# A post-norm decoder layer on one core: the keys of the second attention spread over steps, the projection's bias moved to TensorE, and first waits moved

## What is computed

```python
x = layernorm(x + self_attention(x))            # out @ proj_w.T + proj_b
x = layernorm(x + cross_attention(x, ctx, mask)) # q = x @ Wq.T + bq; k, v from 4 x 77 context rows
x = layernorm(x + moe(x))                       # router, 8 experts, top 2, capacity 1024

# cross attention
qh, kh, vh = heads(q @ Wq.T + bq), heads(k @ Wk.T + bk), heads(v @ Wv.T + bv)
scores = qh @ kh.T / sqrt(16) + mask * NEG
out = softmax(scores) @ vh
return merge(out) @ Wo.T + bo
```

## Time and profile before

| | |
|---|---|
| runs | 1827.96, 1835.07 (median), 1846.97 us |
| profiled execution | 1830.21 us, of which its span is 1828.4 us |
| busy | PE 89%, DVE 70%, PEld 58%, ACT 55%, POOL 21% of the span |
| TensorE clock granted, mean | 0.93 of full |
| DMA | 184 MB, 101 GB/s on the mean |

### The profile page before, as it was taken

How to read it: one execution, slowest core, us unless ns; L and a number is a source line. 1 busy time by engine, 2 the same in 40 slices (tenths; PEclk the granted TensorE clock), 3 DMA queues, 4 the chain that set the end, 5 groups by cost and what they waited for, 6 DMA issues and landing times. The chain is left out here.

```text
span 1828.4 us, 36172 instructions
## 1 busy us (share of the span) xinstructions
PE 1623.4 (89%) x14816; PEld 1061.1 (58%) x14816; DVE 1278.5 (70%) x2240; ACT 1006.9 (55%) x1727; POOL 387.6 (21%) x265
## 2 busy tenths in 40 slices
PE   7869999999999999999777599869984999999990
PEld 6734444444444444444366455547763888888890
DVE  6978888888888888888177446752333677777744
ACT  5326777777777777777635267844532233333313
POOL 6550000000000000000014001101452355555521
PEclk9968999999999999999889578978996999999995
DMA  7955444443433343420238866223213244434226
GB/s 240 259 168 95 93 93 91 91 90 90 98 84 65 63 69 69 69 39 9 78 125 239 191 96 122 68 86 110 84 39 114 70 96 96 96 96 96 39 24 195
DMA packets 130388, 184.36 MB, mean 101 GB/s; under 512 B 29466, under 2 KB 93736, under 8 KB 129132
## 3 DMA queue, kind: packets, MB, share of 16 engines
q1 hardware_dynamic: 113456, 153.70, 34.0%
q0 software_dynamic: 13440, 22.07, 5.8%
q10 hardware_dynamic: 3328, 6.29, 2.1%
HBM read 115.32 MB, written 70.06 MB: 101 GB/s over the span
## 5 line engine op out<-in xcount | busy, mean ns | idle before, releaser
L734 DVE TENSOR_REDUCE att_row_max<-att_ring 128x2 f32<-128x1024 f32 x512 | 601.7, 1220 | 108.4 <-PE att_ring L799 76.4
L718 ACT ACTIVATE att_w_exp<-att_s_ps 128x512 f32<-128x512 f32 x1008 | 539.2, 598 | 210.1 <-PE att_s_ps L846 140.3
L873 PE MATMUL att_a_ps<-att_w_exp,att_v_group 128*32 128x512 f32 x2048 | 273.6, 606 | 0.8 <-ACT att_acc_sb L707 0.6
L832 PE MATMUL att_s_ps<-att_q_stack,att_k_stack 62*128 62x512 f32 x640 | 183.8, 478 | 0.0
L832 PEld LDWEIGHTS att_s_ps<-att_q_stack,att_k_stack 62*128 62x128 f32 x640 | 86.2, 184 | 122.2 <-ACT att_w_exp L718 111.9
L2357 ACT ACTIVATE ex_hid<-ex_h_ps,ex_b 128x512 f32<-128x512 f32 x128 | 87.4, 686 | 116.7 <-DVE ex_h_lo L2412 66.5
L2412 DVE TENSOR_TENSOR ex_h_lo<-ex_hid,ex_h_hi 128x512 fp32r<-128x512 f32 x128 | 138.6, 1083 | 4.4
L648 POOL COPY att_eyes<-keep_slope_eye 128x384 bf16<-128x384 bf16 x16 | 8.1, 507 | 622.6 <-PE att_s_ps L846 613.7
L2307 POOL DMA_INDIRECT x_scr<-ex_y,ex_home x60 | 100.6, 1677 | 176.0 <-DVE ex_y L2402 162.3
L846 PE MATMUL att_s_ps<-att_eyes,keep_past_bf 64*128 64x64 bf16 x3786 | 131.8, 193 | 0.0
L799 PE MATMUL att_ring<-att_k_stack,att_q_stack 60*128 60x512 f32 x640 | 125.6, 439 | 5.0 <-DVE att_row_max L734 4.1
(11 more groups left out here) (314 smaller groups left out, 3552.6 us busy)
## 6 DMA issues: line engine op xcount, KB each, us to landing
first_w_raw<-ew SPq DMA_DIRECT2D x16, 1024.0 KB
att_k_stack<-qk_scr SPq DMA_DIRECT2D x40, 256.0 KB
rows_scr<-att_zeros POOLq DMA_DIRECT2D x8, 1040.0 KB, 9.3
first_rows<-rows_scr SPq DMA_DIRECT2D x16, 520.0 KB
qk_scr<-qkv_t_lo SPq DMA_DIRECT2D x14, 512.0 KB, 4.7
qk_scr<-qkv_t_hi SPq DMA_DIRECT2D x14, 512.0 KB, 4.4
keep_k_stack<-qk_scr SPq DMA_DIRECT2D x24, 256.0 KB
att_q_stack<-qk_scr SPq DMA_DIRECT2D x20, 256.0 KB
```

Of the source, the lines that this page charges most:

```text
L718: nc.scalar.activation(w_exp[(STEPS * g.n + st) % SETS][h][:, :], score_bank(v), ACT.Exp).then_inc(exp_done, 1)
L734: nc.vector.tensor_reduce(out, ring[place.slot][:, :, :], AX.X, ALU.max).then_inc(ring_free, 1)
L832: ins = nc.tensor.matmul(score_bank(v), ks[g.buf][rows, c, j, kt * P:(kt + 1) * P], qs[g.buf][rows, j, c * CH:(c + 1) * CH], start=True, s ...
L873: ins = nc.tensor.matmul(a_ps[32 * h:32 * h + 32, :], vg[g.buf][:, kt, h * VW:h * VW + 32], w_exp[(STEPS * g.n + st) % SETS][h][:, :], sta ...
```

## The change

Five edits:

1. The projection's bias is no longer added by POOL. `proj_b` is loaded as rows 0 and 64 of a tile of 128 rows that is otherwise zero, split in hi and lo on DVE in step 0, and added by a 25th matmul per 128 tokens, ones (128 rows) times the parts. `bias_x` goes, in the attention stage too (with ACT's wait for the load of `x`).
2. Keys: two per step at the end of PE's steps 3 to 6, in the two banks of `t1_ps`; PE first waits for `x1_lo_done` of the same step. The values are made in step 8 in `r_ps`, taken in step 9; `wv` is split in step 7, the keys are shifted in steps 7 and 8. DVE does `split_keys` ahead of `residual(0)` in step 1, and the mask parts (`make_masks`) at the end of step 2. The context and its weights are loaded ahead of `x` of chunk 1.
3. The mask's tiles have 128 rows, not 64.
4. `q_out` lives on into `stage_cross`: the wait for the last query stores goes from the end of `stage_self_out` to DVE behind its 14 maxima, and to each later `load_stack`. `move_top(0)` is issued ahead of the second `load_ones`, of `load_x(0)` and of `bo`.
5. In the experts' stage the waits for `const_in` go from the head of PE's and ACT's streams to ACT behind the first `split_x` and to DVE's first `shares`.

```diff
@@ stage_attention
-            pool.tensor_tensor(lent["x"], lent["x"], lent["proj_b"].unsqueeze(1).to_broadcast([P, TPC, C]), ALU.add)
...
-            act.wait_ge(io["chunk_in"][0], 16)
@@
-KEY_BANKS = 4
-MASK_ROWS = 64
+KEY_BANKS = 2
+KEY_STEPS = range(3, 7)
+MASK_ROWS = 128
@@ load_projection
-    sp.dma_start(lent["proj_b"], io["proj_b"].partition_broadcast(P)).then_inc(lent["weights_in"], 16)
+    sp.dma_start(lent["proj_b"], io["proj_b"]).then_inc(lent["weights_in"], 16)
@@ stage_self_out, sync
-            for n in range(1, LOADED):
-                load(n)
-                if n == 1:
-                    load_keys()
...
+            sp.dma_start(att[1][:, :, :], chunk_rows(io["att_scr"], 1)).then_inc(in_done[1], 16)
+            load_keys()
+            sp.dma_start(x[1], chunk_rows(io["x"], 1)).then_inc(in_done[1], 16)
+            load(2)
+            load_masks()
+            load(3)
...
-                if n == 0:
+                if n == 3:
                     load_ones(sp, io, stacks[0], ones_in)
-                if n == 2:
+                if n == 6:
                     sp.wait_ge(k_done, PAIRS)
                     load_ones(sp, io, stacks[1], ones_in)
-                if n in (5, 7):
+                if n in (4, 6):
                     first_side(sp, n // 2 - 2, 0)
             sp.wait_ge(ones_in, 64)
             for c in range(2):
                 sp.wait_ge(x1_out[c], 16 * CHUNKS // 2)
-                sp.wait_ge(q_out[c], Q_STORES * CHUNKS // 2)
@@ gpsimd
-            def bias_x(n):
...
+            pool.memset(all_ones[:, :].bitcast(F32), 1.0).then_inc(pool_step, 1)
@@ scalar
+                if step in KEY_STEPS:
+                    for j in range(2):
+                        take_keys(2 * (step - KEY_STEPS[0]) + j)
+                if step == 7:
+                    act.wait_ge(weights_in, 112)
+                    nc.scalar.activation(wv_hi[:, :, :], wv_raw[:, :, :], ACT.Copy).then_inc(key_hi, 1)
+                if step in (7, 8):
+                    for j in range((step - 7) * PAIRS // 2, (step - 6) * PAIRS // 2):
                         shifted_keys(j)
@@ vector
+                if step == 0:
+                    dve.wait_ge(weights_in, 80)
+                    nc.vector.tensor_copy(proj_parts[:, :], proj_b).then_inc(prep, 1)
+                    dve.wait_ge(prep, 3)
+                    nc.vector.tensor_tensor(proj_parts[64:128, :], proj_b[64:128, :], proj_parts[64:128, :].bitcast(F32), ALU.subtract).then_inc(prep, 1)
+                if step == 1:
+                    split_keys()
                 if mid is not None:
                     residual(mid)
                     moments(mid)
-                if step == 1:
-                    split_keys()
...
+                if step == 2:
+                    make_masks()
+                if step in KEY_STEPS:
+                    for j in range(2):
+                        key_parts(2 * (step - KEY_STEPS[0]) + j)
@@ tensor
                              for a, b in parts3(a_hi[n % 2], a_lo[n % 2], w_hi, w_lo)]
+                    prods.append((all_ones[:, :], proj_parts[:, :]))
...
-                if step in (1, 2):
-                    for j in range((step - 1) * KEY_BANKS, step * KEY_BANKS):
-                        keys(j)
                 if old is not None:
-                    if old == 0:
-                        pe.wait_ge(k_taken, KEY_BANKS + 2)
                     transpose_x1(old)
-                if step == 2:
+                if last is not None:
+                    queries(last)
+                if step in KEY_STEPS:
+                    pe.wait_ge(x1_lo_done, old + 1)
+                    for j in range(2):
+                        keys(2 * (step - KEY_STEPS[0]) + j)
+                if step == 8:
                     for i in range(2):
                         make_values(i)
@@ stage_cross, sync
+            load_ones(sp, io, qst[2], ones_in)
             load_stack(2)
-            for i in (2, 3):
-                load_ones(sp, io, qst[i], ones_in)
+            move_top(0)
+            sp.wait_ge(ones_in, 96)
+            load_ones(sp, io, qst[3], ones_in)
             load_x(0)
-            move_top(0)
@@ vector, behind the 14 maxima
+            for c in range(2):
+                dve.wait_ge(q_out[c], Q_STORES * CHUNKS // 2)
@@ stage_experts
-            act.wait_ge(const_in, 32)
...
             split_x(0, 0)
+            act.wait_ge(const_in, 32)
...
+                if h == 0:
+                    dve.wait_ge(const_in, 32)
...
-            pe.wait_ge(const_in, 32)
```

More of the change, by code:

```diff
@@ L1040, in cross_tiles @@
             "v_all": s.sb("v_all", [L, B, H, VP], F32), "key_bias": s.sb("key_bias", [L, B], F32),
-            "stacks": [s.sb(f"q_stack{i}", [P, PAIRS, CH], F32R) for i in range(2)]}
+            "stacks": [s.sb(f"q_stack{i}", [P, PAIRS, CH], F32R) for i in range(2)],
+            "q_out": [s.sem(f"q_out{i}") for i in range(2)]}
 def load_query_side(eng, io, n, side, stack):
@@ L1080, in stage_self_out @@
         q_sum = [s.sb(f"q_sum{i}", [P, CK, CH], F32) for i in range(2)]
-        q_hi = [s.sb(f"q_hi{i}", [P, CK, CH], F32R) for i in range(2)]
-        q_lo = [s.sb(f"q_lo{i}", [P, CK, CH], F32R) for i in range(2)]
         norm = Norm(nc, s, io["apart"])
@@ L1094, in stage_self_out @@
         k_high = [s.sb(f"k_high{i}", [P, B * L], F32R) for i in range(KEY_BANKS)]
[L1096 removed]
+        k_low = [s.sb(f"k_low{i}", [P, B * L], F32)[:, :] for i in range(KEY_BANKS)]
+        proj_parts, all_ones = s.sb("proj_parts", [MASK_ROWS, C], F32R), s.sb("all_ones", [MASK_ROWS, P], F32R)
         k_max, k_exp, v_all, key_bias, stacks = (pre[name] for name in ("k_max", "k_exp", "v_all", "key_bias", "stacks"))
@@ L1100, in stage_self_out @@
         wk_hi, wk_lo = [spare[:, i * 2048:(i + 1) * 2048].rearrange("p (c m) -> p c m", c=CK) for i in range(2)]
+        q_hi = [s.sb(f"q_hi{i}", [P, CK, CH], F32R) for i in range(2)]
+        q_lo = [s.sb(f"q_lo{i}", [P, CK, CH], F32R) for i in range(2)]
         t_ps = s.pb("t_ps", (P, CK, CH))
@@ L1104, in stage_self_out @@
         q_ps = s.pb("q_ps", (P, CK, CH))
-        key_banks = [bank[:, i, 0:B * L] for bank in (t1_ps, q_ps) for i in range(2)]
+        key_banks = [t1_ps[:, i, 0:B * L] for i in range(KEY_BANKS)]
         ctx_in, mask_in, weights_in = s.sem("ctx_in"), s.sem("mask_in"), lent["weights_in"]
@@ L1119, in stage_self_out @@
         x1_out = [s.sem(f"x1_out{i}") for i in range(2)]
-        q_out = [s.sem(f"q_out{i}") for i in range(2)]
+        q_out = pre["q_out"]
         block = s.block()
@@ L1265, in _ @@
                     split_keys()
-                if step == 2:
-                    for j in range(KEY_BANKS, PAIRS):
-                        take_keys(j)
                 if old is not None:
@@ L1272, in _ @@
                     norm.take_root(act, mid)
-                if step == 1:
-                    for j in range(KEY_BANKS):
-                        take_keys(j)
-                    act.wait_ge(weights_in, 112)
-                    nc.scalar.activation(wv_hi[:, :, :], wv_raw[:, :, :], ACT.Copy).then_inc(key_hi, 1)
                 if last is not None:
@@ L1282, in _ @@
                     split_q(last)
-                if step in (4, 5):
-                    for j in range((step - 4) * PAIRS // 2, (step - 3) * PAIRS // 2):
+                if step in KEY_STEPS:
[6 more added lines that the diff above has]
+                    for j in range((step - 7) * PAIRS // 2, (step - 6) * PAIRS // 2):
                         shifted_keys(j)
-                if step in (6, 8):
-                    first_side(act, step // 2 - 3, 1)
+                if step in (5, 7):
+                    first_side(act, step // 2 - 2, 1)
         @block.vector
@@ L1450, in make_values @@
                     for j, (x, y) in enumerate(prods):
-                        ins = nc.tensor.matmul(q_ps[0:L, i, k * C:(k + 1) * C], x, y, start=(j == 0), stop=(j == len(prods) - 1))
+                        ins = nc.tensor.matmul(r_ps[0:L, b, :], x, y, start=(j == 0), stop=(j == len(prods) - 1))
                 ins.then_inc(k_done, 1)
@@ L1459, in _ @@
                     project(mid)
-                if step in (1, 2):
-                    for j in range((step - 1) * KEY_BANKS, step * KEY_BANKS):
-                        keys(j)
                 if old is not None:
-                    if old == 0:
-                        pe.wait_ge(k_taken, KEY_BANKS + 2)
                     transpose_x1(old)
-                if step == 2:
+                if last is not None:
[5 more added lines that the diff above has]
+                if step == 8:
                     for i in range(2):
                         make_values(i)
-                if last is not None:
-                    if last == 0:
-                        pe.wait_ge(k_step, PAIRS + 2)
-                    queries(last)
 LEAD = 14
```

60 lines of the change are left out of this document (30 added, 30 removed).

## The result

The changed kernel takes 1824.66 us (median of 20 runs, 1818.57 to 1837.77) against 1832.64 before (20 runs); the ratio is 0.9949, 95% interval 0.9930 to 0.9969. It is faster by half a per cent, 9.3 us by the ratio and 8.0 by the two medians, where I had forecast 21.3. The profiled execution's span is 1817.2 us instead of 1828.4.

What follows compares the result with a forecast made beforehand. A chain of waits between TensorE and VectorE was taken to set the self-output stage's step, VectorE the plain steps. Gains of 14.7, 4.4 and 2.2 made 21.3 us: 1835.1 to 1813.8 us, range 1801 to 1828.

Steps and rivals of the forecast that it cites:

- Steps 1 and 2: Self-output stage: first x1 4.4 us earlier; with keys two per step at 11.1 us intervals, last residual 9.2 us earlier.
- rival B: Self-output stage: TensorE's clock falls once in the new gaps, costing 6.5 us; 14.8 gained, 1820.3 us; chance 0.13.
- The tail of part 2: Self-output stage behind the last residual: 4.7 MB in 16.7 us, last split waiting 2.3 us for a store (0 to 6).
- Step 3: Boundary to second attention: first matmul 0.9 us behind the last issue, 5.5 us gained, 14.7 with the 9.2 before it.
- Step 4: Second attention's first shifts: scores 18.4 us behind the stage's start instead of 22.8; gain 4.4, bounds 0 and 5.57.
- Steps 3 and 4: Boundary and second attention's first shifts together: 5.5 and 4.4 us, 9.9 us gained.
- Step 5: Experts' stage: TensorE starts with the stage, 2.2 us gained, bounds 0 and 2.25.
- rival A: Last split and first shifts: the queues give half the gain back; 13.2 us gained, 1821.9 us; chance 0.20.
- the gap of step 3: Self-output stage's third step: TensorE has nothing to do from about 933.6 to 937.4, before the first keys.

Runs made afterwards that it cites:

- the projection's run: Changed kernel with the boundary's waits and load order and the experts' waits put back as before; ratio to the kernel before 0.9940 (0.9920-0.9960).
- the dense fill: Changed kernel with loads in the old order, idle matmuls before the last chunk's scores and throughout the second attention's start; ratio to the kernel before 1.0136 (1.0105-1.0168).

## Why the prediction was right in its sign and wrong in its size

- **Steps 1 and 2, right.** The weight pieces (1.82 us for 1.9), x1 of chunk 0, the pair's 2.2 us (2.09), the interval of 11.1 (11.07) and the last residual (984.86 for 984.7) came as worked out. From the stage's own start, which came 0.9 us earlier, the gain is 8.1 of the 9.2: the first pair ran mostly at half clock, 3.2 us instead of 2.1, as rival B had it. The two key parts take 2.96 us beside GpSimd's split instead of 1.1, hidden, since the loop has room there. What the Trainium skill says ("SBUF — State Buffer", "Who interferes with whom") applies to the key parts too, where I had not used it: in the kernel before they did not lie beside such an operation. The experiments put this part at 0.9940 alone, all of the change's gain.
- **The tail of part 2, the first wrong term.** I let the last split wait 2.3 us and gave it up to 6; it waited 4.37. The rate was right and the bytes were not. From the issue of the store of x1(6) to the end of that wait the queues moved 271 GB/s, where I had 281 (the last two columns are the DMA share and GB/s; changed kernel):

```profile
984.35:1005.40 21.05, 13.57 (x79) 11.12 (x77) 10.54 (x26) 11.36 (x19) 5.20 (x2) 0.92 1.01 271
```

  That is 5.7 MB, where I had counted 4.7. The seventh chunk's queries, 1 MB, are issued at 999.06 and 999.46, before the wait ends, and I had left them out; that they are the missing megabyte fits and was not tested.

- **Step 3, half right.** The first matmul does follow the last issue by 0.56 us (I had 0.9), and the first maxima moved by 11.9 in all: 14.7 less the 2.0 us by which that wait grew, and most of the 1.1 missing at the last residual. Alone the edit gave 6.2 where I had 5.5. What failed is the belief that an earlier first matmul is kept: first maxima 11.9 us earlier, third shift store 9.3.
- **Step 4, wrong.** "18.4 behind the start" needed the first exchange of shifts to take 3.2 us, as the third chunk's does with nothing ahead; I had read that one only, and the fourth's and fifth's take 5.3 to 6.5 in both kernels. The other terms held (the store 10.91 behind the start, the scores 4.34 behind the second issue). The exchange took 6.56 with one stack ahead, as rival A had said, and the moved loads then stood ahead of the second exchange, 14.06 us. That the wait would be there I had in no step: I followed the first chunk's exchange past the moved loads and never the second's. Steps 3 and 4, 9.9 us in the sum, were worth 1.2 in the two traces at the third shift store and nothing that shows in the ratios. Where stacks are loaded the engines are as busy as in the tail and move less, and that was in no term either. Windows of the changed kernel:

```profile
1010.00:1020.00 10.00, 9.56 (x78) 8.32 (x76) 7.62 (x11) 0.44 (x1) 0.00 (x0) 0.50 1.05 193
...
1030.00:1040.00 10.00, 8.71 (x52) 5.00 (x52) 2.82 (x5) 6.08 (x10) 0.00 (x0) 0.50 1.08 136
```

- **Step 5, right in kind.** 2.2 expected; 2.1 at the first matmuls, 1.7 kept on the mean of the profiles.
- **The rivals.** A is what happened, less of it at the first scores (12.9 us kept, by A 11.0) and more behind them: its 13.2 us would have been 1821.9. B's clock fell behind the gap of step 3 and was back by 940.9; its larger part, half-clock stretches later in the second attention that take 3 to 4 us from one execution and not from the next, was in no step. They widen every comparison of traces here: from the third to the eighth store it took 104.8 us before, 101.5 after and 118 in the projection's run, all with the same code, at a mean granted clock of 0.93, 0.98 and 0.80.

Rival A's rule stands in the Trainium skill too ("DMA: Bandwidth & Descriptors", "Queues, rings and completion order"): a DMA's completion lands only behind every earlier write of the same DMA engine, whichever queue it came from. The exchanges agree: 64 KB are confirmed, by the issue of the reload, after 3.3 us at the third chunk, where little is in flight, 6.6 behind one stack, 9.1 with 512 KB more, 14.1 behind the next stack, tile and rows. I had not drawn on it in the forecast; it spoke against step 4. The queues are not full to the end of an exchange, though: in the changed kernel's first the DMA share was 1.02 in its first microsecond, about 0.3 in the third and fourth and 0.1 in the sixth, so that it is a few of the 16 engines that are waited for.

That the amount of traffic sets the first scores is borne out by adding to it, in one trace; that less traffic would bring them forward was not tried. Why the clock is down from the stage's start to somewhere between 1063 and 1109, in the dense fill with TensorE busy throughout the first 40 us, and what decides when it rises, stays open.

## What to carry to other kernels

Before an earlier start is counted, list what stands in the DMA queues between it and each transfer that the next stage waits for, for the second and third turn as well as the first; where the engines are full there, an earlier start or another order moves the wait and earns nothing. When edits are summed, sum them at a point behind the common bottleneck: here 0.6, 0.4 and 0.2 per cent alone made 0.5 together. And a gap of 1.68 us of TensorE cost 1.5 or 5.5 us here, by the execution: in three pairs of kernels a dozen idle matmuls in it were worth 0.5, 0.4 and 0.2 per cent. The intervals of each pair overlap; weighted by them the three make 0.3 per cent, 0.1 to 0.5 (an estimate). At a gap behind which the clock fell anyway, a little later, the same means gained nothing.

## What was not expected of the hardware

- In the dense fill the granted clock stood at 0.50 to 0.56 over 40 us (1010 to 1050) in which TensorE was busy in every window (10.00 of 10). Behind a gap of 1.68 us near the stage's end it fell in seven of ten kernels for 3.5 us longer than in the other three, and in none of seven with the gap filled did the stretch take more than 53.0.
- Two operations of 128x308 on VectorE beside GpSimd's subtraction of 128x1024 took 2.96 us, one of them 2.50; before, without it, 0.54 each.
- A 64 KB store and the wait for it took from 1.6 to 15.4 us, by what other transfers were in flight.
- With the same instructions the self-output stage of the kernel before reached its last residual 91.4 or 94.8 us behind its start, by where TensorE's clock rose.
